# Scratch tensors re-laid: features with heads innermost, fewer and longer DMAs, shift rows issued by POOL

## The chip, the cores and the metric

One core of one Trainium2 chip runs the whole kernel. The metric is the device time of one execution in microseconds. TensorE (PE), VectorE (DVE), ScalarE (ACT), GpSimd (POOL) and SyncE (SP) run their own instruction streams and meet by semaphores. DMAs are issued by a queue of SP, ACT or POOL and moved by 16 DMA engines.

## The reference

A decoder layer on 32 sequences of 128 tokens, 128 features, 16 heads of 8. First a linear attention block, then cross attention to 77 context tokens, then a mixture of experts. The change touches the cross attention:

```python
def _feature_map(x, fm_w, fm_b):
    z = jnp.einsum('nshd,ed->nshe', x, fm_w) + fm_b
    return jnp.concatenate([jnp.exp(z), jnp.exp(-z)], axis=-1)   # 16 features per head
...
v, k, q = (_feature_map(x, fm_w, fm_b) for x in (v, k, q))
scores = jnp.einsum('nqhd,nkhd->nhqk', q, k) / jnp.sqrt(jnp.float32(EMBED))
attn = jax.nn.softmax(scores, axis=-1)
out = jnp.einsum('nhql,nlhd->nqhd', attn, v)
out = out.reshape(N, S, HEADS * EXP_DIM)
return out @ fc_w.T + fc_b
```

## The kernel before

`decoder_layer` has four phases, each with one function per engine. Phase 1 is the first attention block. The sequences are taken in groups of four (`JP`, `NG` = 8 groups).

**Phase 2, features.** For each group PE transposes the context and multiplies context and tokens with `map_w`; ACT takes the exponentials of K and then of Q, each as f32 and as bf16, in two halves (`hf`) of 8 heads with 16 features each on the 128 partitions, and copies the values to `vals` (line 547). Each feature is kept as three bf16 parts (high, middle, low): VectorE makes the parts of Q (`qpart`, semaphores `qhi`, `qmid`, `qlo`), POOL those of K (`kpart`; `khi`, `kmid`, `klo`). The buffers exist twice (`par`, the group's parity), so ACT may write a part of group g only when group g-2's DMA has left it (`k_sent`, `q_sent`). SP sends the parts to scratch in DRAM (`qparts`, `kparts`): per group six DMAs for K (line 473: two halves, three parts) and two for Q (line 478), in runs of 616 and 1,024 bytes.

**Phase 3, attention.** Sequences go in pairs (`JA` = 2, `NA` = 16 pairs). The scores are a sum over pairs of parts: `Q_PART` = (0, 0, 0, 1, 1, 2) meets `K_PART` = (0, 1, 2, 0, 1, 0), so 6 x 16 = 96 rows (`ROWS`) of `qst` and `kst`. `load_parts` fills them from scratch, transposed to 16 features on the partitions and heads along the row: per pair six DMAs of 128 KB for Q (line 629, every copy of a part by itself, 16 rows in runs of 512 bytes) and three for K (line 632, runs of 308 bytes). Four buffers (`NBUF`) take turns. PE computes the scores of pair g+2 (line 666, three units of heads) while it attends pair g; VectorE takes the row maxima, splits them in three parts (`parts`), PE turns them (line 675), ACT copies them to `mT` (line 838), and SP copies them as three further rows, the shift rows, to `qst` by two DMAs (line 640). Then PE computes the scores again with 99 rows, which subtracts the maximum (line 696), ACT takes the exponential (line 853), PE multiplies with the values (line 711), turns and projects (lines 728, 734, 740). `body(g)` of PE waits for the shift rows of its pair (`m_in`) and, in its first unit, for the loads of pair g+2 (`parts_in`). POOL copies each sequence's values (line 870) and adds the bias `fcb` to all of `xs` at once (line 874).

SP's order: writes of groups 0 to 5 each behind their context load; then loads of pairs 0 and 1 and the writes of groups 6 and 7 alternately; shift rows of pair 0; loads of pairs 2 and 3; then for each pair the load of pair g+3 (behind `bp`, the scores of pair g-1) and the shift rows of pair g+1. Phase 4, the experts, follows on all engines.

## Time and profile before

| | |
|---|---|
| median of 3 runs | 672.51 us (663.89 to 672.9) |
| the profiled execution | 663.64 us, its span 661.8 us |
| mean granted TensorE clock | 0.863 of 2.4 GHz |
| busy: PE, DVE, ACT, POOL | 474.3, 341.8, 253.9, 190.8 us |
| DMA | 101,485 packets, 61.94 MB, mean 94 GB/s |

Busy times are sums over an engine's instructions. "DMA share" is the mean share of the 16 DMA engines that were moving a packet; it can pass 1 where packets of several queues overlap. "PEclk" is the granted clock as a part of 2.4 GHz.

### The profile page before, as it was taken

Reading aid. Unit: us, or ns where it says so; the run is one execution under the profiler, and the core shown is the slowest. Engines: PE = TensorE matmul, PEld = TensorE weight load, DVE = VectorE, ACT = ScalarE, POOL = GpSimd, SP = SyncE. Lnnn points to the kernel's source line nnn. Section 1 sums busy time; section 2 is a strip of 40 time slices with the busy share of each in tenths; the row PEclk is TensorE's granted clock in tenths of the full one; section 3 lists DMA queues with packets and bytes.
Section 4 is the critical chain, followed back from the end, with each engine's and each line's share of the span. In section 5 each row is a group of like instructions: output and inputs, shape, how many; then the busy total and the mean of one; then the engine's idle time right before and its main releaser. Section 6 shows DMA issues by size and latency. Waiting matters only on the chain.

```text
span 661.8 us, 11782 instructions
## 1 busy us (share of the span) xinstructions
PE 474.3 (72%) x3778; PEld 317.1 (48%) x3778; DVE 341.8 (52%) x969; ACT 253.9 (38%) x578; POOL 190.8 (29%) x223
## 2 busy tenths in 40 slices
PE   0588888777771259998888888859894188988860
PEld 0255555544441136665655656534562055766650
DVE  4567755616759325555675676464830032334343
ACT  0445545358780024333443444536630022323220
POOL 3132222357787000000000000011047600455560
PEclk9999999988885557677987899969897689899895
DMA  5820000003669998989898994000031101556639
GB/s 96 295 76 1 0 0 1 0 11 115 200 190 161 178 122 92 97 90 104 92 119 87 104 113 44 2 1 1 0 125 53 49 0 33 150 178 203 203 102 254
DMA packets 101485, 61.94 MB, mean 94 GB/s; under 512 B 33832, under 2 KB 99656, under 8 KB 101320
## 3 DMA queue, kind: packets, MB, share of 16 engines
q1 hardware_dynamic: 91976, 52.92, 45.9%
q0 software_dynamic: 2560, 5.31, 2.3%
q10 hardware_dynamic: 6912, 3.25, 2.1%
q8 instruction: 19, 0.31, 0.2%
q14 instruction: 18, 0.15, 0.1%
HBM read 40.34 MB, written 20.73 MB: 92 GB/s over the span
## 4 chain that ended last, share of the span: by engine, by line
PE 42%; DVE 15%; SPq 12%; ACT 8%; issue 8%; another core or an unknown queue 6%; DMA 6%; POOL 1%; ACTq 1%; DVEq 0%; POOLq 0%
SPq L473 5%; PE bank L711 4%; PE bank L696 4%; PE bank L1204 3%; PE bank L1214 3%; ACT prob L853 3%; PE bank L1215 2%; PE bank L1263 2%; PE bank L734 2%; DMA qst<-mT 2%; PE bank L740 2%; PE bank L666 2%; PE bank L728 2%; SPq L629 2%
## 5 line engine op out<-in xcount | busy, mean ns | idle before, releaser
L853 ACT ACTIVATE prob<-bank 77x512 f32<-77x512 f32 x128 | 73.5, 591 | 111.6 <-PE bank L696 111.1
L870 POOL COPY vcur<-vals 77x272 f32 (+1 forms) x32 | 13.2, 416 | 192.6 <-PE bank L711 192.6
L711 PE MATMUL bank<-prob,vcur 77*17 77x128 f32 x1024 | 58.6, 305 | 12.5 <-ACT prob L853 12.1
L1178 POOL DMA_INDIRECT routed<-t_y,t_no x48 | 45.9, 956 | 71.6 <-DVE t_y L1047 59.9
L778 DVE TENSOR_REDUCE mx<-bank 128x5 f32<-128x385 f32 (+1 forms) x96 | 53.6, 579 | 24.3 <-PE bank L666 22.4
L666 PE MATMUL bank<-kst,qst 96*128 96x77 bf16 x512 | 40.9, 225 | 32.8 <-DMA kst<-kparts 27.6
L696 PE MATMUL bank<-qst,kst 99*77 99x128 bf16 x512 | 57.9, 244 | 7.8 <-DMA qst<-mT 6.6
L696 PEld LDWEIGHTS bank<-qst,kst 99*77 99x77 bf16 x512 | 44.2, 132 | 18.3 <-issue 9.9
L825 DVE COPY avs_s<-bank 128x512 f32<-128x512 f32 x32 | 22.1, 692 | 59.2 <-PE bank L711 59.2
L941 DVE TENSOR_TENSOR act<-bank,s_g 128x512 f32<-128x512 f32 x24 | 16.5, 688 | 62.9 <-ACT s_g L1115 59.6
L666 PEld LDWEIGHTS bank<-kst,qst 96*128 96x128 bf16 x512 | 31.9, 115 | 35.6 <-DMA kst<-kparts 14.6
L1204 PE MATMUL bank<-sd,act 128*128 128x128 f32 x192 | 27.9, 291 | 28.8 <-DVE act L941 20.0
L1204 PEld LDWEIGHTS bank<-sd,act 128*128 128x128 f32 x192 | 26.4, 203 | 43.1 <-DVE act L941 24.2
L1173 POOL DMA_INDIRECT sorted_in<-h_rows,pos_s x32 | 30.8, 964 | 41.7 <-issue 41.7
L379 POOL TENSOR_TENSOR qkv<-qkv,rn 128x256 f32<-128x256 f32 x32 | 19.1, 629 | 76.4 <-DVE rn L297 76.4
L1115 ACT ACTIVATE s_g<-bank 128x512 f32<-128x512 f32 x24 | 14.2, 597 | 69.0 <-PE bank L1215 33.0
L1040 DVE TENSOR_TENSOR t_act<-bank,t_sg 128x128 f32<-128x128 f32 x48 | 14.0, 291 | 48.4 <-ACT t_sg L1132 24.5
L1128 ACT COPY t_hT<-bank 128x128 f32<-128x128 f32 x48 | 12.7, 265 | 57.2 <-PE bank L1254 31.8
L711 PEld LDWEIGHTS bank<-prob,vcur 77*17 77x17 f32 x1024 | 17.5, 99 | 35.7 <-ACT prob L853 23.6
L1263 PE MATMUL bank<-t_hT,t_w 128*128 128x128 f32 x96 | 21.9, 311 | 13.5 <-ACT t_hT L1128 9.1
L331 ACT ACTIVATE xn<-xs,ln_bias,ln_rstd 128x128 f32<-128x128 f32 (+1 forms) x64 | 26.4, 482 | 10.1 <-DVE ln_bias L279 9.8
L412 PE MATMUL bank<-wqkv,xnT 128*128 128x384 f32 x64 | 25.3, 543 | 5.7 <-ACT xnT L338 5.7
(178 smaller groups left out, 1066.6 us busy)
## 6 DMA issues: line engine op xcount, KB each, us to landing
qst<-qparts SPq DMA_DIRECT2D x96, 128.0 KB, 5.3
t_w<-in_expert_w SPq DMA_DIRECT2D x48, 192.0 KB
qparts<-qpart SPq DMA_DIRECT2D x16, 384.0 KB, 3.4
kparts<-kpart SPq DMA_DIRECT2D x48, 77.0 KB
kst<-kparts SPq DMA_DIRECT2D x16, 231.0 KB, 7.8
sorted_in<-fill SPq DMA_DIRECT2D x1, 3168.0 KB, 10.4
t_row<-sorted_in ACTq DMA_DIRECT2D x48, 66.0 KB
kst<-kparts SPq DMA_DIRECT2D x16, 154.0 KB, 8.1
```

The source lines that it names most:

```text
L331: i = a.activation(dst[:, j], x_of(g, j), ACT.Identity, scale=ln_rstd[k][:, j:j + 1], bias=ln_bias[k][:, j:j + 1])
L412: pe.matmul(bank[1 + j][:, 0:3 * D], xnT[par][:, j * P:(j + 1) * P], wqkv[:], start=True, stop=True).then_inc(s["qkvp"], 1)
L473: sp.dma_start(kparts[a, :, heads, bass.ds(g * JK, JK)].rearrange("e h t -> h e t"), kpart[par][hf][:, a]).then_inc(k_sent[par][hf], 16)
L666: i = pe.matmul(bank[n % 2][:, (h - h0) * KEYS:(h - h0 + 1) * KEYS], qst[r][0:ROWS, h, j * S:(j + 1) * S], kst[r][0:ROWS, h, j * KEYS:(j + ...
L696: i = pe.matmul(bank[2 + u % 2][0:KEYS, c * S:(c + 1) * S], kst[r][0:SHIFT_ROWS, h, j * KEYS:(j + 1) * KEYS], qst[r][0:SHIFT_ROWS, h, j * ...
L711: i = pe.matmul(bank[4][32 * c:32 * c + EX + 1, (u - 1) * P:u * P], av_lhs(g, r, j, 4 * (u - 1) + c), prob[(u - 1) % 2][:, c], start=True, ...
L778: v.tensor_reduce(mx[:, n // 3, h0:h1], bank[n % 2][:, 0:(h1 - h0) * KEYS].rearrange("p (h k) -> p h k", k=KEYS), AX.X, ALU.max).then_inc( ...
L853: a.activation(prob[u % 2][:].rearrange("p c t -> p (c t)"), bank[2 + u % 2][0:KEYS], ACT.Exp, scale=SCORE_SCALE).then_inc(s["expd"], 1)
L1173: p.indirect_dma_start(out=sorted_in, out_offset=bass.IndirectOffsetOnAxis(ap=pos[:, b:b + 1].bitcast(U32), axis=0), in_=h_rows[:, b], in_ ...
L1178: p.indirect_dma_start(out=routed, out_offset=bass.IndirectOffsetOnAxis(ap=t_no[r][:].bitcast(U32), axis=0), in_=t_y[r][:], in_offset=None ...
L1204: i = pe.matmul(bank[BK_DOWN[par]][:, j * D:(j + 1) * D], act[c][:, j * P:(j + 1) * P], sd[:, c], start=(c == 0 and j == 0), stop=(c == CH ...
L1263: pe.matmul(bank[2 + r % 2][:, 0:P], t_w[r][:, 0:FF], t_hT[r % 2][:], start=True, stop=True)
```

## The change

The features are laid out with heads innermost: partition = feature x 16 + head, the first half (`hf` = 0) all the exp(z), the second all the exp(-z). The host builds `fm_wT`, `fm_b`, `signs` and `signcol` for it, and the copy of the values in line 547 reads its bank with a stride of 16 elements. The scratch tensors get a leading dimension for the group, then part, feature, head, token. So a write of a half with all its parts is one DMA (4 per group), and a row of 16 heads is contiguous: 16 KB for Q and 9,856 bytes for K. `qst` and `kst` hold four sequences instead of two, in three buffers instead of four, the third in the memory of the feature stage's own buffers (`early`); that one may be filled only after all writes have left and PE's last transposes of that stage (`vp`). A load of a group is three DMAs for Q, in which the copies of a part come from one broadcast source, and three for K. SP loads group 0 at turns 2 (Q) and 3 (K) of the feature stage and group 1 at turns 5 and 6, group 2 behind all writes, group G behind the scores of group G-3. The shift rows go to POOL's queue, ahead of the value copies; the bias is added by sequence; a memset of the third buffer's rows of ones is done by POOL between the first and the second shift. The loops of SP in the feature stage and of all engines in attention are written out.

```diff
-    NBUF = 4
+    NBUF = 3
...
-        qparts = nc.dram_tensor("qparts", (HEADS, EX, PARTS, TOK), BF16).ap()
-        kparts = nc.dram_tensor("kparts", (PARTS, EX, HEADS, B * KEYS), BF16).ap()
+        qparts = nc.dram_tensor("qparts", (NG, PARTS, EX, HEADS, GT), BF16).ap()
+        kparts = nc.dram_tensor("kparts", (NG, PARTS, EX, HEADS, JK), BF16).ap()
...
+            def body(g):
+                par = g % 2
+                for hf in range(2):
                     sp.wait_ge(s["klo"], g * 2 + (hf + 1))
-                    for a in range(PARTS):
-                        sp.dma_start(kparts[a, :, heads, bass.ds(g * JK, JK)].rearrange("e h t -> h e t"),
-                                     kpart[par][hf][:, a]).then_inc(k_sent[par][hf], 16)
+                    sp.dma_start(kparts[g, :, hf * HD:(hf + 1) * HD].rearrange("a e h t -> (e h) a t"),
+                                 kpart[par][hf][:]).then_inc(k_sent[par][hf], 16)
                 for hf in range(2):
-                    heads = slice(hf * HALF, (hf + 1) * HALF)
                     sp.wait_ge(s["qlo"], g * 2 + (hf + 1))
-                    sp.dma_start(qparts[heads, :, :, bass.ds(g * GT, GT)].rearrange("h e a t -> (h e) a t"),
+                    sp.dma_start(qparts[g, :, hf * HD:(hf + 1) * HD].rearrange("a e h t -> (e h) a t"),
                                  qpart[par][hf][:]).then_inc(q_sent[par][hf], 16)
...
+            for g in range(NG):
+                if g < NG - 2:
+                    sp.wait_ge(s["ctxTp"], g + 1)
+                    ctx_load(g + 2, g % 2)
+                if g == 2:
+                    sent(0, 1)
+                    load_q(sp, 0)
+                if g == 3:
+                    load_k(sp, 0)
+                if g == 5:
+                    sent(1, 2)
+                    load_q(sp, 1)
+                if g == 6:
+                    load_k(sp, 1)
+                body(g)
...
+        stage = [sb3, sb3, early()]
+        qst = [place(f"qst{i}", [SHIFT_ROWS, HEADS, GT], BF16) for i, place in enumerate(stage)]
+        kst = [place(f"kst{i}", [SHIFT_ROWS, HEADS, JK], BF16) for i, place in enumerate(stage)]
...
-        def load_parts(sp, g, r):
-
+        def load_q(sp, group):
+
+            r = group % NBUF
             for at, part, n in Q_RUNS:
-                for i in range(n):
-                    sp.dma_start(qst[r][(at + i) * EX:(at + i + 1) * EX],
-                                 qparts[:, :, part, bass.ds(g * JA * S, JA * S)].rearrange("h e t -> e h t")).then_inc(parts_in[r], 16)
+                same = qparts[group, part].rearrange("(o e) h t -> o e h t", o=1).broadcast_to([n, EX, HEADS, GT])
+                sp.dma_start(qst[r][at * EX:(at + n) * EX], same).then_inc(parts_in[r], 16)
+
+        def load_k(sp, group):
+
+            r = group % NBUF
             for at, part, n in K_RUNS:
                 sp.dma_start(kst[r][at * EX:(at + n) * EX],
-                             kparts[part:part + n, :, :, bass.ds(g * JA * KEYS, JA * KEYS)].rearrange("a e h t -> (a e) h t")).then_inc(parts_in[r], 16)
+                             kparts[group, part:part + n].rearrange("a e h t -> (a e) h t")).then_inc(parts_in[r], 16)
...
+            all_sent(sp, NG // 2)
+            sp.wait_ge(s["vp"], NG)
+            load_q(sp, 2)
+            load_k(sp, 2)
+            for group in range(3, NG):
+                sp.wait_ge(s["bp"], (group - 2) * (2 * 4 * JA))
+                load_q(sp, group)
+                load_k(sp, group)
...
+            shift(0)
             p.wait_ge(s["xn2"], NG)
-            p.tensor_tensor(xs[:], xs[:], fcb[:].rearrange("p (o f) -> p o f", o=1).broadcast_to([P, B, D]),
-                            ALU.add).then_inc(s["xb2"], 1)
+            for b in range(2 * JA):
+                add_bias(b)
+            all_sent(p, NG // 2)
+            p.wait_ge(s["vp"], NG)
+            p.wait_ge(s["xb2"], 2 * JA)
+            p.memset(kst[NBUF - 1][ROWS:SHIFT_ROWS], 1.0).then_inc(s["ones_rows"], 1)
+            p.wait_ge(s["ones_rows"], 1 + NBUF)
+            for g in range(NA):
+                if g < NA - 1:
+                    shift(g + 1)
+                for j in range(JA):
+                    b = g * JA + j
+                    if b + 2 * JA < B:
+
+                        p.wait_ge(s["avp"], 4 * (b + 1))
+                        copy_values(b + 2 * JA, b % (2 * JA))
+                        add_bias(b + 2 * JA)
```

`shift(g)` on POOL waits for `mT` of pair g and issues the same two DMAs as SP's did; `home(g, j)` gives a pair's buffer and place in it.

## Rows read from the trace of the kernel before

**Rows 1.** The page's chain that ended last, shares of the span by engine

```profile
PE 42%; DVE 15%; SPq 12%; ACT 8%; issue 8%; another core or an unknown queue 6%; DMA 6%; POOL 1%; ACTq 1%; DVEq 0%; POOLq 0%
```

**Rows 2.** Windows: busy us (x instructions) per engine, granted clock, DMA share, GB/s

```profile
144.00:200.00 56.00, 41.05 (x156) 24.68 (x156) 32.89 (x44) 44.98 (x89) 42.00 (x48) 0.86 0.51 154
200.00:239.00 39.00, 6.81 (x69) 4.68 (x69) 21.40 (x27) 0.95 (x3) 11.40 (x6) 0.51 1.14 171
239.00:437.40 198.40, 172.70 (x2315) 121.04 (x2315) 118.64 (x344) 85.18 (x175) 11.48 (x28) 0.84 0.80 83
384.00:400.00 16.00, 12.74 (x206) 9.07 (x207) 10.77 (x31) 7.19 (x16) 1.23 (x3) 1.00 1.19 113
```

**Rows 3.** The chain in order of time: start us, us, what

```profile
151.39 0.81 SPq L473
...
198.50 0.34 SPq L629
...
231.81 7.19 DMA kst<-kparts
```

**Rows 4.** Timeline of ACT, groups 4 and 7: start us, us, instruction

```profile
171.99 0.46 ACT L538 COPY ctxT_s<-bank 128x308 f32<-128x308 f32 x1
...
173.89 0.51 ACT L534 ACTIVATE kpart<-bank,map_b 128x308 bf16<-128x308 f32 x1
...
199.03 1.06 ACT L547 COPY vals<-bank 77x512 f32 x2
```

**Rows 5.** Timeline of SP, the K writes of group 1

```profile
159.26 4.79 SPq L473 DMA_DIRECT2D kparts<-kpart  x6
```

**Rows 6.** Window in attention: granted clock, DMA share, GB/s

```profile
276.00:286.00 10.00, 0.50 1.02 101
```

**Rows 7.** Waits between 250 and 437 us: us in total, times, longest

```profile
PE bank L696 <- DMA qst<-mT: 3.8, 5, 1.0
```

**Rows 8.** Timeline of ACT, the copies of the shift rows

```profile
217.85 0.27 ACT L838 COPY mT<-bank 128x128 bf16<-128x128 bf16 x1 [17.75 <-PE bank L675]
...
243.12 0.27 ACT L838 COPY mT<-bank 128x128 bf16<-128x128 bf16 x1 [0.98 <-PE bank L675]
...
386.30 0.27 ACT L838 COPY mT<-bank 128x128 bf16<-128x128 bf16 x1 [1.68 <-PE bank L675]
397.50 0.27 ACT L838 COPY mT<-bank 128x128 bf16<-128x128 bf16 x1 [0.58 <-PE bank L675]
...
418.63 0.27 ACT L838 COPY mT<-bank 128x128 bf16<-128x128 bf16 x1 [0.82 <-PE bank L675]
```

**Rows 9.** Short windows in a K write, a Q write, a shift copy: clock, DMA share, GB/s

```profile
154.20:154.30 0.10, 1.00 0.51 154
...
158.20:158.40 0.20, 1.00 0.95 353
...
420.40:420.50 0.10, 1.00 0.24 54
```

**Rows 10.** Window in a write of rows of 25 KB, the same columns

```profile
30.00:31.00 1.00, 1.00 0.94 406
```

**Rows 11.** The page's DMA issues: KB each, median us from issue to landing

```profile
qparts<-qpart SPq DMA_DIRECT2D x16, 384.0 KB, 3.4
```

**Rows 12.** Timeline of PE, the scores of pairs 0 and 1

```profile
211.04 0.88 PE L666 MATMUL bank<-kst,qst 96*128 96x77 bf16 x11 [13.43 <-DMA kst<-kparts]
...
224.44 0.90 PE L666 MATMUL bank<-kst,qst 96*128 96x77 bf16 x11 [6.63 <-DMA kst<-kparts]
225.74 2.28 PE L666 MATMUL bank<-kst,qst 96*128 96x77 bf16 x21 [0.41 <-DVE mx L778]
```

**Rows 13.** Single lines of POOL and ACT

```profile
L1178 POOL DMA_INDIRECT routed<-t_y,t_no x48: 952/957/960, 565.4 to 643.6; - x48
...
L547 ACT COPY vals<-bank x16: 573/593/624, 151.2 to 199.5; 77x512 f32 x12, 77x512 f32<-77x512 f32 x4
...
131.56 8.76 POOL L587 MEMSET kst<- 3x2464 bf16 x4
```

More of the change, by code:

```diff
@@ L525, in act_phase2, with features @@
         def act_phase2(a):
-            def features(g, par, g2, hf, z, f, part, zp, f_done, hi_done, lo, sent, loads):
+            def features(g, par, g2, hf, z, f, part, zp, f_done, hi_done, lo, sent):
                 a.wait_ge(s[zp], g * 2 + (hf + 1))
@@ L803, in tail @@
                 if stage == 2:
-                    if is_first(g) and j == 0:
-                        v.wait_ge(s["xb2"], 1)
+                    v.wait_ge(s["xb2"], b + 1)
                     v.wait_ge(s["fcp"], b + 1)
```

160 lines of the change are left out of this document (70 added, 90 removed).

## The prediction

> **What bounds the kernel now.** I read the chain that ended last first. No engine holds it: TensorE has 42% of the span, and SP's issuing 12%, an unusually large share for a queue [rows 1]. Then I cut the span into stages. Feature stage (144 to 200 us): ACT is busy for 45 of 56 us, VectorE for 33, POOL for 42. From 200 to 239 us TensorE does 6.8 us of work in 39. Attention (239 to 437.4) has TensorE busy for 173 of 198 us [rows 2]; the mixture of experts behind it takes the other 224 us and is not touched. The chain in order of time says what the 39 us are: SP starts line 473 at 151.4 and does not catch up; the first loads go out at 198.5, and the last that attention needs lands at 239 [rows 3]. ACT starts group 4 at 172.0 and ends group 7 at 200.1 with its last copy, 7.0 us per group of four sequences [rows 4]. SP takes 4.8 us for a group's six K writes, 0.8 each [rows 5]; with Q's two, the context load and waits it is 7.9 from the first group's start to the second's [rows 3, 5]. So the lag of SP's queue holds TensorE from about 200 to 239. In attention the DMA engines are full too (1.02 busy, 101 GB/s [rows 6]), but PE waits for DMA there in few places: 3.8 us for shift rows in the 16 pairs [rows 7]. The copies of the shift rows, one per pair of sequences, mark the pace: 11.2 us where the clock of 2.4 GHz is granted (1.00 from 384 to 400 [rows 2]); from 243.1 to 418.6 the mean of 14 pairs is 12.5 us, 25 per group [rows 8], with a mean clock of 0.84 [rows 2].
>
> **Part 1, the writes: 8 DMAs per group become 4.** SP per group: 4 of 0.8 us instead of 8 [rows 5], 3.2 us against ACT's 7.0. SP leaves the path; ACT's 7.0 us pace is left and the stage itself gains nothing that I count. What comes back is the lag afterwards. The new writes have 128 rows as outermost dimension, in runs of 1,024 and 616 bytes as before, so the bytes cost no more.
>
> **Part 2, the loads, and this is where I think the change fails.** A load of three copies of one part is one DMA whose source is (3 copies, step 0) x 16 rows x 16 KB, and the two-copy one has 2 outermost. How many of the 16 DMA engines does such a DMA use? The rows of before answer by shape. While only scratch writes of K run (outermost dimension 8 heads), a tenth of a microsecond shows 0.51 of the engines busy, half of 16; a Q write (outermost 128) shows 0.95 at 353 GB/s; the shift rows (3 destination rows outermost) show 0.24, 3 to 4 engines [rows 9]. So the outermost count limits the engines: three engines move 786 KB, and two move 524 KB. A rule speaks against this very form. The Trainium skill ("DMA: Bandwidth & Descriptors", section "Rules for kernel authors") says that a leading zero-stride broadcast of c copies confines the DMA to at most c engines, and its section "Why a DMA increments its semaphore by 16 and not by 1" says that these are the lowest-numbered ones. The trace's half and quarter agree; by that rule the sum is the one below, without it rival (b).
>
> What does the busiest engine carry for a group? One part is 16 x 16 KB = 262 KB. It carries one copy of the three, one of the two, 1/16 of the single one (16 KB), and 1/16 of K's 946 KB (59 KB). That both DMAs begin at the same engine no row shows; I take it, since one queue cuts up both, and a start elsewhere takes the two-copy share off (rival (a)). Rate of one engine: at best 406/(0.94 x 16) = 27 GB/s [rows 10]; where three engines each write one row of SBUF it is 54/(0.24 x 16) = 14 GB/s [rows 9]; with 16 engines on 16 rows it is 101/(1.02 x 16) = 6.2 [rows 6], but then 101 GB/s in total, which two or three engines don't reach, so I leave that out. I take 14 for the three-engine DMA, the nearest row, and 27 for the two-engine one, whose rows are long (16 KB against 256 bytes): 18.7 + 9.7 + 0.6 + 2.2 = 31.2 us per group. Both at 27: 22.2. Both at 14: 40.2. The Trainium skill ("SBUF — State Buffer", section "Door 1: The DMA port swizzle") puts partitions 32 apart on the same port, so copies one and three (rows 0 to 15 and 32 to 47) share one port's 27 GB/s and the two-copy DMA does not; an estimate from that page is 19.3 + 9.7 us in place of 18.7 + 9.7. No row shows it by itself. A load lands about 2.3 us after its bytes (a Q write lands in 3.4 [rows 11], of which 384 KB at 353 GB/s are 1.1).
>
> *In the feature stage.* The loads go into the same queue as the writes, ahead of them. The Q load of group 0 is issued in turn 2, about 163 (group 1's writes start at 159.3 [rows 5], and 4 take 3.2 us). It fills the first engine for 18.7 + 9.7 + 0.6 = 29 us. Group 2's writes, just behind, land at 163 + 29 + 2.3 = 194. Group 4's K features use the same buffer and wait for that: ACT wanted it at 173.9 [rows 4]. Delay 20 us, and behind ACT wait VectorE, POOL and TensorE. Then again: the Q load of group 1 goes out about 8 us after ACT resumes (202), the writes of group 5 behind it land at 202 + 29 + 2.3 = 234, and group 7's features, due at 194 + 3 x 7 = 215, wait for them. ACT ends the stage at 234 + 5 = 239 instead of 200.
>
> *At the start of attention.* Scores of the first pair start at 211.0 and its shift rows are copied at 217.9 [rows 8, 12]; the second pair takes 3.6 us more (224.44 to 228.02 [rows 12]); with 1 us for the shift rows' landing 11.5 us, so attention starts at 250. But group 2's load waits for all writes (239 + 5 = 244) and takes 31.2 + 2.3 + 0.5 to issue: 278. The scores of group 2 are due at the first pair of group 1, at 250 + 25 = 275. So group 1 starts at 278.
>
> *In attention.* Load G is issued when group G-3's last scores with shift are done, which I put 1.5 us ahead of group G-2's start (the last of eight score blocks of 11.2/8 us), and is needed when group G-1 starts: one group of time, 25 us, and this 1.5, against 33.5. Not hidden: groups 2 to 6 each start 33.5 - 1.5 = 32 us after the one before, 5 x 32 = 160, so group 6 starts at 438. From there to the end before took from about 393.4 (4.1 ahead of the copy at 397.5, as between 239.0 and 243.1 [rows 3, 8]) to 437.4, 44 us. End of attention 482, some 44 us later than before.
>
> **Part 3, shift rows on POOL.** Two issues per pair leave SP and go to POOL. The trace has no direct copy there; the nearest row is an indirect one, 957 ns [rows 13]. 1.9 + 2.3 = 4.2 us from copy to landing, against 11.2 - 4.1 = 7.1 between the copy and the next pair. POOL has 11 us of work in the 198 of attention [rows 2], and what queues behind it, the value copies, is wanted a pair later. No cost; at best the 3.8 us of waits [rows 7] go. If the cover goes, each microsecond late costs 15.
>
> **Part 4, the rest.** The bias add on POOL becomes 32 pieces; VectorE waits for a piece that is four sequences ahead: nothing. A memset twice as long as before, 4.4 us (8.76 for four [rows 13]), stands on POOL before the second shift, hidden by the first pair. The copy of values reads PSUM with a stride of 16 elements; the contiguous one takes 593 ns [rows 13]. No row shows such a read on ACT; from 0 to twice the time, 1.2 us per group or 9.5 us; I take 0, hidden by the stalls above. Unrolled loops: 0 to -3 us. Heads innermost is renamed columns otherwise.
>
> **Sum.** 663.6 (span 661.8 and 1.8 around it) + 44 = 708 us for the profiled execution. The median of the runs is 672.5, 9 us above that; part of this lies outside the stretches that the loads would set, so I give 712.
>
> **Rivals.** (a) The few engines run at 27 GB/s each, or the two broadcast DMAs fall on different engines (18.7 + 0.6 + 2.2 = 21.5 us). Group 4 waits to 185, the stage ends at 221, attention starts at 233; a load takes 24.5 us against 25, just hidden; 233 + 198 = 431, 6 us earlier than before: 657. For it: long rows, and the 14 comes from 256-byte ones. Against: it is the best row of the trace, and leaves no reserve. The point from which the load decides is 24 us on the busiest engine. (b) The change does what it says: the loads spread over 16 engines (a lowering that puts the 16 rows outside would do it). Then the stage ends at about 199, attention starts at 211 and lasts 198: 409, 28 us earlier, 635, or 630 with less waiting. Against it stand all three shapes [rows 9]. (c) 14 GB/s for both: first stall to 203, stage end near 259, load 42.5 us, 5 x 41: 782. (d) Shift rows issued on POOL are late, by 3 us a pair if an issue costs 3 us: 45 us on top of (b), hidden in my forecast. The Trainium skill ("SBUF — State Buffer", section "SBUF: two separate sides") warns that POOL can't write its descriptors while VectorE holds the shared port; no row here shows a direct copy on POOL.
>
> **How the numbers follow.** Forecast, with 27 to 34 us per group on the busiest engine, 690 to 736: 0.52. (a) 0.20; between (a) and the forecast 0.05; (b) 0.14; (c) 0.07; (d) 0.02. From 652 to 736 only (b), (c) and edges are left out, 2 in 10. A measurement of this kernel tells 2% from no change. Faster by more than that: (b) and an edge of (a), 0.18. Within: the rest of (a), 0.20. Slower: 0.62.
>
> **What would show it.** Windows during a Q load in attention: a DMA share of 0.2 or less at 40 to 60 GB/s, where before it was 1.02 at 101. ACT idle for some 20 us near 174 to 194, ended by a K write. TensorE waiting 6 to 8 us at the start of each of groups 1 to 6, ended by a DMA. I am wrong if the DMA share stands near 1 with over 150 GB/s during loads (b), or if the waits are there in the feature stage but not in attention (a).

## The result and the profile after

The changed kernel takes 739.65 us (median of 4 runs, 734.32 to 744.69); the kernel before, on the same chip, 669.61 (4 runs, 663.89 to 672.9). The ratio is 1.106 with a 95% interval of 1.093 to 1.118: slower, as forecast, but above the range, which ended at 736. Some executions of this program, whatever the kernel, are some per cent longer at a lower granted clock: medians here are over all runs, ratios and their intervals compare only the others. The profiled execution took 744.69 us, 742.9 of it span; the forecast for it was 708. So 33 us of loss are missing in the sum beside the 44 it had, and some 3 us lie behind attention (227.5 us against 224.4).

The page's chain that ended last, after; against [rows 1] SP's issuing falls from 12% to 2% and DMA rises from 6% to 19%:

```profile
PE 42%; DMA 19%; DVE 11%; ACT 8%; another core or an unknown queue 7%; issue 6%; POOL 4%; SPq 2%; ACTq 1%; DVEq 0%; POOLq 0%
```

Windows of the same stages (columns as in [rows 2]): features, the gap before attention, attention from its first score matmul with shift rows:

```profile
144.00:243.80 99.80, 42.95 (x158) 26.61 (x156) 36.07 (x45) 44.88 (x89) 42.95 (x47) 0.71 0.53 141
243.80:266.80 23.00, 5.99 (x65) 4.27 (x65) 15.83 (x26) 0.27 (x1) 11.35 (x13) 0.50 0.70 154
266.80:515.40 248.60, 215.75 (x2319) 151.01 (x2319) 121.13 (x343) 87.07 (x176) 41.29 (x86) 0.64 0.26 58
```

The feature stage lasts 100 us instead of 56 with the same busy time of ACT (44.9 against 45.0). What was 39 us of SP's lag is 23. Attention lasts 249 us. Before, it was 198 from 239.0, or 207 from its first score matmul with shift rows at 230.85, behind which TensorE waited 7.6 us for the K rows of pair 2. Its DMA share fell from 0.80 to 0.26, and TensorE's granted clock from 0.84 to 0.64.

ACT's timeline, where [rows 4] shows no such stop (idle before and its releaser in brackets), and the first copies of the shift rows (compare [rows 8]):

```profile
195.67 0.52 ACT L545 ACTIVATE kpart<-bank,map_b 128x308 bf16<-128x308 f32 x1 [22.01 <-DMA kparts<-kpart]
239.20 0.52 ACT L545 ACTIVATE kpart<-bank,map_b 128x308 bf16<-128x308 f32 x1 [21.75 <-DMA kparts<-kpart]
242.75 1.05 ACT L558 COPY vals<-bank 77x512 f32 x2
252.10 0.27 ACT L851 COPY mT<-bank 128x128 bf16<-128x128 bf16 x1 [8.30 <-PE bank L688]
271.34 0.27 ACT L851 COPY mT<-bank 128x128 bf16<-128x128 bf16 x1 [0.98 <-PE bank L688]
286.60 0.27 ACT L851 COPY mT<-bank 128x128 bf16<-128x128 bf16 x1 [1.44 <-PE bank L688]
302.87 0.27 ACT L851 COPY mT<-bank 128x128 bf16<-128x128 bf16 x1 [1.44 <-PE bank L688]
```

SP's timeline shows the cause of these two stops from the queue's side. The Q loads of groups 0 and 1 are issued in 2 us each. Then the issue of the next two Q writes, each 0.65 us in the median, takes 25 and 24 us together: SP itself is held up behind a load. Below them are the Q loads of groups 2, 3 and 4:

```profile
162.73 2.01 SPq L650 DMA_DIRECT2D qst<-qparts  x3
166.87 25.02 SPq L482 DMA_DIRECT2D qparts<-qpart  x2
...
206.77 1.85 SPq L650 DMA_DIRECT2D qst<-qparts  x3
211.06 23.96 SPq L482 DMA_DIRECT2D qparts<-qpart  x2
...
252.17 1.87 SPq L650 DMA_DIRECT2D qst<-qparts  x3
294.75 1.84 SPq L650 DMA_DIRECT2D qst<-qparts  x3
328.79 1.84 SPq L650 DMA_DIRECT2D qst<-qparts  x3
```

Windows of 2 us in the stall of group 4 and during the load of group 3, issued at 294.75 (granted clock, DMA share, GB/s):

```profile
176.00:178.00 2.00, 1.00 0.21 57
302.00:304.00 2.00, 0.50 1.01 179
308.00:310.00 2.00, 1.00 0.20 59
310.00:312.00 2.00, 1.00 0.17 49
326.00:328.00 2.00, 0.50 0.05 21
```

Some 10 us after the issue all engines are still full, and K pieces go through. Then 0.17 to 0.20 of 16 engines are left, that is three, at 49 to 59 GB/s in all, and at the end one (0.05 of 16). The trace's semaphore events give the last landing of each load: 330.4 for this one, 35.7 us after its issue; over the six loads in attention it is 34.9 to 36.5 us.

PE's timeline holds what my sum had as nothing: the scores with shift wait for the shift rows, at pair 0 and at the second pair of each of groups 1 to 5 (pairs 3, 5, 7, 9, 11). The copy for that second pair is issued some 9 us after the group's load. The chain in order of time has the same transfers with their whole length, issue to landing:

```profile
266.81 0.65 PE L709 MATMUL bank<-qst,kst 99*77 99x128 bf16 x4 [11.34 <-DMA qst<-mT]
...
314.74 0.64 PE L709 MATMUL bank<-qst,kst 99*77 99x128 bf16 x4 [3.25 <-DMA qst<-mT]
...
349.88 0.65 PE L709 MATMUL bank<-qst,kst 99*77 99x128 bf16 x4 [4.30 <-DMA qst<-mT]
...
383.93 0.65 PE L709 MATMUL bank<-qst,kst 99*77 99x128 bf16 x4 [6.23 <-DMA qst<-mT]
```

```profile
253.52 13.24 DMA qst<-mT
...
304.05 10.65 DMA qst<-mT
...
338.08 11.76 DMA qst<-mT
...
372.15 11.74 DMA qst<-mT
```

In total (waits of the whole span: us, times, longest) it is 32.3 us, against 3.8 in [rows 7], which leave out the first pair (6.6 with it):

```profile
PE bank L709 <- DMA qst<-mT: 32.3, 6, 11.3
```

No matmul of attention waits for a load. But the loads of groups 3, 4 and 5 land at 330.4, 364.3 and 399.8 us, and TensorE needs them when groups 2, 3 and 4 start, at 331.0, 366.2 and 400.2: the loads are only just hidden.

So there were two things to test. My theory, call it A: the broadcast loads on few engines explain the loss. A rival, call it B (the expectations below use A and B in senses of their own, given there): the shift rows, now beside the loads on another queue instead of in order with them on SP's, are late, and would be even with loads on all engines.

### The profile page after: what moved, and what is told of

Same layout as the page of the kernel before. It is cut to its first block, busy times and chain, and to the rows that moved or that the text cites. A ratio compares the mean times of both kernels' runs of the same rounds, so it can differ in the third digit from the quotient of the medians.

```text
span 742.9 us, 10825 instructions
## 1 busy us (share of the span) xinstructions
PE 517.3 (70%) x3778; PEld 347.9 (47%) x3778; DVE 342.2 (46%) x969; ACT 254.8 (34%) x578; POOL 221.3 (30%) x285
## 4 chain that ended last, share of the span: by engine, by line
PE 42%; DMA 19%; DVE 11%; ACT 8%; another core or an unknown queue 7%; issue 6%; POOL 4%; SPq 2%; ACTq 1%; DVEq 0%; POOLq 0%
DMA qst<-mT 9%; DMA kparts<-kpart 8%; PE bank L709 6%; PE bank L724 5%; PE bank L679 3%; PE bank L741 3%; PE bank L753 3%; PE bank L1239 2%; PE bank L747 2%; ACT prob L866 2%; PE bank L1298 2%; PE bank L1249 2%; PE bank L1250 2%; DVE ss L290 1%
## 5 line engine op out<-in xcount | busy, mean ns | idle before, releaser
L866 ACT ACTIVATE prob<-bank 77x512 f32<-77x512 f32 x128 | 75.0, 592 | 153.7 <-PE bank L709 153.7
L709 PE MATMUL bank<-qst,kst 99*77 99x128 bf16 x512 | 70.8, 284 | 32.3 <-DMA qst<-mT 32.3
L709 PEld LDWEIGHTS bank<-qst,kst 99*77 99x77 bf16 x512 | 55.6, 161 | 46.1 <-DMA qst<-mT 33.5
L724 PE MATMUL bank<-prob,vcur 77*17 77x128 f32 x1024 | 69.9, 358 | 9.2 <-ACT prob L866 8.2
L1213 POOL DMA_INDIRECT routed<-t_y,t_no x48 | 46.0, 958 | 75.3 <-DVE t_y L1082 64.2
L893 POOL DMA_DIRECT2D qst<-mT x32 | 19.7, 618 | 120.4 <-ACT mT L851 120.4
L679 PE MATMUL bank<-kst,qst 96*128 96x77 bf16 x512 | 49.1, 254 | 5.9 <-DVE mx L792 3.6
L1239 PEld LDWEIGHTS bank<-sd,act 128*128 128x128 f32 x192 | 26.4, 203 | 44.6 <-DVE act L976 23.7
L570 DVE TENSOR_TENSOR res_q<-qkv,qpart 128x512 f32<-128x512 f32 x16 | 14.9, 935 | 67.2 <-ACT qpart L545 67.1
L679 PEld LDWEIGHTS bank<-kst,qst 96*128 96x128 bf16 x512 | 40.6, 136 | 7.8 <-DVE mx L792 5.3
L530 PE MATMUL bank<-ident_s,kf 128*77 128x128 f32 x64 | 10.2, 312 | 41.3 <-ACT kf L542 41.3
L883 POOL COPY vcur<-vals 77x272 f32<-77x272 f32 x32 | 14.2, 448 | 81.3 <-PE bank L724 81.2
```

The lines of the kernel that those rows point to most:

```text
L679: i = pe.matmul(bank[n % 2][:, (h - h0) * KEYS:(h - h0 + 1) * KEYS], qst[r][0:ROWS, h, c * S:(c + 1) * S], kst[r][0:ROWS, h, c * KEYS:(c + ...
L709: i = pe.matmul(bank[2 + u % 2][0:KEYS, c * S:(c + 1) * S], kst[r][0:SHIFT_ROWS, h, t * KEYS:(t + 1) * KEYS], qst[r][0:SHIFT_ROWS, h, t * ...
L724: i = pe.matmul(bank[4][32 * c:32 * c + EX + 1, (u - 1) * P:u * P], av_lhs(g, j, 4 * (u - 1) + c), prob[(u - 1) % 2][:, c], start=True, st ...
L866: a.activation(prob[u % 2][:].rearrange("p c t -> p (c t)"), bank[2 + u % 2][0:KEYS], ACT.Exp, scale=SCORE_SCALE).then_inc(s["expd"], 1)
L893: p.dma_start(qst[r][ROWS:SHIFT_ROWS, :, c * S:(c + 1) * S], mT[g % 2][at:at + PARTS * HEADS]).then_inc(m_in[r], 16)
L1213: p.indirect_dma_start(out=routed, out_offset=bass.IndirectOffsetOnAxis(ap=t_no[r][:].bitcast(U32), axis=0), in_=t_y[r][:], in_offset=None ...
```

## The experiments

They ran in five sets, on chips on which the kernel before takes 630.46, 680.48, 632.16, 673.86 and 679.96 us; each ratio is to the kernel before of the same set, and times of different sets are not compared. Each edit is to the changed kernel unless another is named. A kernel with one run has a ratio without an interval. The changed kernel itself came to 1.106 on one chip and 1.079 on another, so ratios of different sets can differ by 0.03 for that reason alone. Changes to semaphore counts that follow from an edit are left out of the cuts. The expectation written before each run stands ahead of its result. "Landing" is the median and the longest time from issue to landing of the 32 shift-row DMAs.

**Set 1: where the copies stand, and whose queue.**

*Each copy its own DMA*, 16 feature rows outermost:

```diff
-                same = qparts[group, part].rearrange("(o e) h t -> o e h t", o=1).broadcast_to([n, EX, HEADS, GT])
-                sp.dma_start(qst[r][at * EX:(at + n) * EX], same).then_inc(parts_in[r], 16)
+                for i in range(n):
+                    sp.dma_start(qst[r][(at + i) * EX:(at + i + 1) * EX], qparts[group, part]).then_inc(parts_in[r], 16)
```

> The changed kernel with each copy of a Q part loaded by a DMA of its own (six Q DMAs per group instead of three, outermost dimension 16 rows; all else as in the changed kernel). Theory A (the broadcast source with 3 or 2 copies outermost confines the load to 3 or 2 DMA engines; that makes the stalls of the feature stage, the late shift rows and the slow attention): no stall of ACT near 174 us, DMA share near 1 during a load at 100 GB/s or more, a load done within 20 us, attention starts near 212 us, time 630 to 650 us. Rival B (the long rows or the group-wise buffers themselves are slow, or the shift rows on POOL's queue are late by that queue): the stalls remain, time stays above 700 us.

Measured: 687.27 us, 1.080 (1.066 to 1.095). The stops of ACT for K writes fall from 44.5 to 17.7 us, the longest from 22.0 to 8.2, but shift rows land after 2.7 (median) to 14.9 us, and the waits for them grow from 32.3 to 46.6. The time lies between what the two theories gave.

*The same bytes with the feature row outermost and the copies inside it*:

```diff
-                same = qparts[group, part].rearrange("(o e) h t -> o e h t", o=1).broadcast_to([n, EX, HEADS, GT])
+                same = qparts[group, part].rearrange("e (o h) t -> e o h t", o=1).broadcast_to([EX, n, HEADS, GT])
...
-                             kparts[group, part:part + n].rearrange("a e h t -> (a e) h t")).then_inc(parts_in[r], 16)
+                             kparts[group, part:part + n].rearrange("a e h t -> e a h t")).then_inc(parts_in[r], 16)
```

> The changed kernel with the same six loads per group, but the rows of qst and kst ordered feature first and copy second, so that each load's source has the 16 features outermost and the copies inside. Same bytes, same number of DMAs, same run lengths. Theory A (engine count set by the outermost dimension): as good as single copies or better, since 48 rows are written at once: load at 200 GB/s or more, done in some 12 us, time 625 to 645 us. Rival B (a broadcast source or long runs are slow by themselves): above 700 us.

Measured: 659.81 us, 1.046 (1.035 to 1.058). Windows during its load, issued at 264.45, and PE's timeline at the same load:

```profile
270.00:272.00 2.00, 1.00 0.99 197
278.00:280.00 2.00, 0.91 0.94 193
280.00:282.00 2.00, 0.50 0.22 36
```

```profile
236.50 0.65 PE L709 MATMUL bank<-qst,kst 99*77 99x128 bf16 x4 [10.37 <-DMA qst<-mT]
...
283.43 0.65 PE L709 MATMUL bank<-qst,kst 99*77 99x128 bf16 x4 [5.42 <-DMA qst<-mT]
```

So the outermost count does limit the engines: with 16 outside, the share goes from 0.2 to about 1 and the rate from 49 to 59 to between 113 and 197 GB/s (windows from 266 to 280), and the load lands 18.8 us after its issue instead of 35.7. The stops of ACT are down to 13.4 us, the longest 5.9. The first attention matmul comes at 236.5 instead of 266.8. This is the rule that the Trainium skill states in "DMA: Bandwidth & Descriptors", "Rules for kernel authors" (a leading zero-stride broadcast of c copies uses at most c engines); the share of 0.17 to 0.20 with three copies agrees. But the kernel is still slower than before, above the 625 to 645 us expected, and PE waits 29.3 us for shift rows: theory A doesn't hold alone.

*Shift rows issued from ACT's queue* instead of POOL's, loads as changed:

```diff
                 a.copy(mT[g % 2][:], bank[5][:, 256:256 + S // 2].bitcast(BF16)).then_inc(s["mT"], 1)
+                a.wait_ge(s["mT"], g + 1)
...
+                    a.dma_start(qst[r][ROWS:SHIFT_ROWS, :, c * S:(c + 1) * S], mT[g % 2][at:at + PARTS * HEADS]).then_inc(m_in[r], 16)
```

> The changed kernel with the shift rows issued from ACT's queue right behind the copy, instead of from POOL's. Theory A (the shift rows land late because their 256-byte pieces share DMA engines with 16 KB pieces of the load and take turns with them): they land as late as before, 10 to 13 us behind the issue during a load, time 730 to 750 us. Rival C (POOL's software queue is what makes them late): they land within 4 us, attention starts 10 us earlier and each group of four is some 2 to 5 us shorter, time 705 to 720 us.

Measured (one run): 835.96 us, 1.326. No theory had this time. PE waits for shift rows in 64.2 us between 200 and 460, the longest at the first pair:

```profile
292.70 0.65 PE L709 MATMUL bank<-qst,kst 99*77 99x128 bf16 x4 [31.50 <-DMA qst<-mT]
```

So POOL's queue alone is not what makes them late: another queue made it worse. The packets in the traces say more. On ACT's queue the two copies of a pair go as 96 packets of 256 bytes on three engines, and behind the load they leave one by one: from 288.2 us on, the packets start 0.63 us apart, the time that the fastest of the load's 16 KB packets take (0.61 us). So each small piece lets one large piece go first, which is the turn-taking that theory A of this run names, only much dearer than its 10 to 13 us. The shift rows arrive with the end of the load: TensorE goes on at 292.7 and 359.2 us, the loads' last landings are at 294.2 and 359.3. On POOL's queue the same two copies are six packets of 4,096 bytes and 26 of 64, and 32 of 4 bytes besides, that is 16 for each DMA. So the two queues cut the same copy differently, and this run changes more than the queue.

*Each Q load cut in four by heads*, copies still outermost:

```diff
+                for h in range(0, HEADS, 4):
+                    same = qparts[group, part, :, h:h + 4].rearrange("(o e) h t -> o e h t", o=1).broadcast_to([n, EX, 4, GT])
+                    sp.dma_start(qst[r][at * EX:(at + n) * EX, h:h + 4], same).then_inc(parts_in[r], 16)
```

> The changed kernel with each Q load cut in four by heads, so that one piece is 4 KB instead of 16 KB; still on 3 and 2 engines, same bytes. Theory A (shift rows wait for one piece of the load per piece of their own): they land about 4 times sooner, in some 5 us instead of 12 during a load; attention starts near 258 us instead of 267; a load still takes some 32 us, so the groups still follow each other at 32 to 33 us at best: time 715 to 735 us. Rival (the load's duration alone sets the pace and the shift rows only end last by the profile): 735 to 750 us, unchanged.

Measured (one run): 680.0 us, 1.079. That is 35 us below the range expected. Waits for shift rows fall to 5.8 us, landing 3.1 to 10.4; 16.0 us of waits for K loads come in. Smaller pieces or the slower issue (13 us for a Q load's twelve DMAs) help the shift rows even on few engines.

**Set 2: without shift rows at all.** The kernel before and the changed one were run again on this chip.

> The kernel before, unchanged, for its profile on the chip of this set. Both theories: attention in some 190 to 205 us, the granted clock of TensorE 0.8 or more in it, pairs of 11 to 13 us.

> The changed kernel, unchanged, timed on the chip of this set, since chips differ. Ratio to the kernel before 1.09 to 1.13, as on the first chip.

Measured: 676.26 us and 733.35 (1.079, 1.071 to 1.088). Both expectations were missed by a little: the kernel before had a clock of 0.78 in attention, and the ratio lies below 1.09 and clear of the first chip's interval. The start of attention is the same as on that chip (266.8), but attention takes 233 us there at a clock of 0.73, against 249 at 0.64. So some 15 us of the first result go with the clock that was granted. The changed kernel waits here 24.6 us for shift rows and 11.0 for K loads:

```profile
PE bank L709 <- DMA qst<-mT: 24.6, 6, 11.1
PE bank L679 <- DMA kst<-kparts: 11.0, 3, 6.1
```

*No shift copies*. These two kernels leave the three shift rows out of the scores, so that the softmax has no maximum taken off, and scale the exponent by 1/1000:

```diff
-                                          kst[r][0:SHIFT_ROWS, h, t * KEYS:(t + 1) * KEYS],
-                                          qst[r][0:SHIFT_ROWS, h, t * S:(t + 1) * S], start=True, stop=True)
+                                          kst[r][0:ROWS, h, t * KEYS:(t + 1) * KEYS],
+                                          qst[r][0:ROWS, h, t * S:(t + 1) * S], start=True, stop=True)
...
-                pe.wait_ge(m_in[home(g, 0)[0]], shifts(g))
...
-                    p.dma_start(qst[r][ROWS:SHIFT_ROWS, :, c * S:(c + 1) * S], mT[g % 2][at:at + PARTS * HEADS]).then_inc(m_in[r], 16)
```

> The changed kernel without the copies of the shift rows and without TensorE's wait for them (the second scores take 96 rows, so the maximum is not subtracted, and the exponential is taken at a thousandth of the scale so that it stays finite; POOL still waits for the same copy of ACT). The loads on 3 and 2 engines are left. Theory A (late shift rows cost some 13 us at the start of attention and about 5 per group; behind them the load itself, 33 us against one group of time, limits the pace): start some 12 us earlier, groups still 31 to 33 us apart, 15 to 30 us less than the changed kernel. Rival (the shift rows only end last and the load would hold everything as long): within 8 us of the changed kernel. Rival (the shift rows alone make attention slow): 50 us or more less.

Measured (one run): 725.53 us, 1.066, only 8 us below the changed kernel's median and 2.5 below its fastest run, so the rival of my expectation (within 8 us) held. The load itself is what comes next (waits between 200 and 460, and PE's timeline at the first of them; the load was issued at 253.50):

```profile
PE bank L679 <- DMA kst<-kparts: 35.7, 3, 15.6
```

```profile
294.10 0.57 PE L679 MATMUL bank<-kst,qst 96*128 96x77 bf16 x6 [10.32 <-DMA kst<-kparts]
```

The waits are the same in sum, 35.7 us against 24.6 + 11.0: they only moved from the shift rows to the load. Attention starts at 256.4 instead of 266.8 and ends 5 us earlier.

*No shift copies and the feature outermost*, both edits above:

> The loads of the run with features outermost (16 engines), and the shift rows left out as in the run without shift rows. Theory A (with loads on 16 engines only the shift rows' lateness is left): no wait of TensorE for a DMA in attention, pairs of 11 to 12 us at full clock, attention in some 180 to 190 us, 5% or more below the kernel before. Rival (something else, such as the granted clock by itself, keeps pairs at 15 us): attention in 230 us and more, above the kernel before.

Measured (one run): 657.93 us, 0.967. Nothing in attention waits for a DMA, and its first matmul comes at 222.34:

```profile
222.34 0.63 PE L709 MATMUL bank<-qst,kst 96*77 96x128 bf16 x4
```

So there are two costs that lie one above the other: with few engines the load holds attention and the late shift rows add little; with 16 engines the load is hidden and the shift rows hold it, from 0.967 to 1.046 (ratios of two sets). In the two profiles attention ends 43 us later with shift rows: it starts 14 us later, waits 19 us more inside, and the other 10 go with a lower clock, which no run takes apart from the waits.

**Set 3: what makes the shift rows late.** All but the last are edits to the kernel with the feature outermost.

*Every load cut in four by heads*, 24 DMAs per group with pieces of 4 KB or less:

```diff
+                for h in range(0, HEADS, 4):
+                    same = qparts[group, part, :, h:h + 4].rearrange("e (o h) t -> e o h t", o=1).broadcast_to([EX, n, 4, GT])
...
+                for h in range(0, HEADS, 4):
...
+                                 kparts[group, part:part + n, :, h:h + 4].rearrange("a e h t -> e a h t")).then_inc(parts_in[r], 16)
```

> Features outermost (16 engines), and each load cut in four by heads: pieces of 4 KB for Q and 2.4 KB for K, 24 DMAs per group, the shift rows from POOL as in the changed kernel. Theory A (a shift row's piece waits for one piece of the load at each turn): shift rows land within 5 to 6 us during a load instead of 12, TensorE's waits for them shrink to 0 to 2 us, ratio to the kernel before 0.97 to 1.00 (features outermost alone: 1.046). Rival (it is the load's burst as a whole and not the size of its pieces): they land with the end of the load as before, ratio 1.03 to 1.06.

Measured: 615.07 us, 0.973 (0.962 to 0.985): below the kernel before, though the interval doesn't exclude a gain under 2%. Landing 2.9 to 7.4 us, waits for shift rows 7.0. The issue of a load is now spread over 15 us (SP's timeline), and from 229 to 420 us, inside attention, the clock is 0.80:

```profile
252.28 7.01 SPq L651 DMA_DIRECT2D qst<-qparts  x12
259.34 7.70 SPq L658 DMA_DIRECT2D kst<-kparts  x12
```

```profile
229.00:420.00 191.00, 170.89 (x2226) 120.34 (x2218) 113.62 (x334) 80.75 (x168) 41.30 (x86) 0.80 0.45 75
```

*The load waits until the next pair's shift rows have landed*:

```diff
                 sp.wait_ge(s["bp"], (group - 2) * (2 * 4 * JA))
+                g = 2 * (group - 2)
+                sp.wait_ge(m_in[home(g + 1, 0)[0]], shifts(g + 1))
                 load_q(sp, group)
```

> Features outermost, and SP holds each group's load back until the shift rows of the next pair have landed, so that only one of a group's two shift copies can meet a load. Theory A: shift rows land in 2 to 3 us at the first pair, but the load then runs into the second one's copy or ends late: between the two, ratio 0.98 to 1.03. Rival (shift rows are late for another reason): 1.04 or more.

Measured: 639.86 us, 1.016 (1.008 to 1.024), as expected; waits 13.2 us in place of 29.3, landing 2.8 to 10.4.

*The shift rows row by row*, six DMAs per pair with 16 heads outermost in place of two with 3 rows outermost:

```diff
+                    for a in range(PARTS):
+                        p.dma_start(qst[r][ROWS + a:ROWS + a + 1, :, c * S:(c + 1) * S],
+                                    mT[g % 2][at + a * HEADS:at + (a + 1) * HEADS]).then_inc(m_in[r], 16)
```

> Features outermost with the long pieces, and the shift rows copied one destination row at a time: six DMAs per pair with 16 heads outermost instead of two with 3 rows outermost, so that each of 16 engines carries one piece of each instead of three engines 16. Theory A (each piece waits its turn behind a long piece, so 16 pieces in a row on an engine make the 10 to 12 us): they land in 3 to 5 us plus 2.5 us more of issuing, no waits of TensorE over 2 us in attention, ratio 0.96 to 0.99, near the run without shift rows (0.97). Rival (the queue serves the software queue only when the load is through): waits as with features outermost alone, 1.04 to 1.06.

Measured: 664.4 us, 1.054 (1.045 to 1.064); landing 1.9 to 15.0, waits 36.4; 0.96 to 0.99 was expected. On more engines they are no sooner there.

*The three-copy load split into two and one* (on the changed kernel; this tests the 14 GB/s of my sum):

```diff
+                for i, m in ((0, 2), (2, 1)) if n == 3 else ((0, n),):
+                    same = qparts[group, part].rearrange("(o e) h t -> o e h t", o=1).broadcast_to([m, EX, HEADS, GT])
+                    sp.dma_start(qst[r][(at + i) * EX:(at + i + m) * EX], same).then_inc(parts_in[r], 16)
```

> The changed kernel with the three-copy load split into a two-copy and a one-copy DMA, so that no three engines write rows 0 to 15 and 32 to 47 at once; the busiest engine carries the same two copies as before. If an engine writes at 14 GB/s only where three write (as in the forecast's sum), the busiest engine's share of a load falls from 31 or more to 22 to 24 us: DMA share near 0.13 at 50 to 54 GB/s (27 per engine) in the middle of a load, groups 27 to 31 us apart instead of 33 to 34, held by the shift rows alone. If the rate of an engine into one row is 14 anyway: share 0.13 at 28 GB/s, a load of 40 us, groups 38 us apart, slower than the changed kernel.

Measured (one run): 676.92 us, 1.071. Window in its load:

```profile
302.00:304.00 2.00, 0.50 0.12 49
```

Two engines (0.12 of 16) carry 49 GB/s, 24.5 each; the three of the changed kernel carried 49 to 59, 16 to 20 each in the mean. Their packets of 16 KB show that the mean is of two kinds: in the changed kernel, between 266 and 270 us, one stream of packets takes 0.61 us each (27 GB/s) and two take mostly 1.25 to 1.30 us (12.6 to 13 GB/s); here, between 298 and 315, both streams mostly take 0.61 to 0.66. So the rates of my expectation hold, but its time for a load doesn't: the busiest engine was to need 22 to 24 us, and the loads in attention land 33.5 to 38.4 us after their issue, the first 10 us with all engines busy. TensorE waits 17.3 us for K loads, where I expected waits for shift rows alone (13.4).

**Set 4: size or time of the pieces.** *Loads cut in two* (as above with 8 heads, 12 DMAs per group):

> Features outermost with each load cut in two by heads: pieces of 8 KB for Q and 4.9 KB for K. Theory A (lateness follows the size of the load's pieces: 16 KB gave up to 12.3 us from issue to landing, 4 KB up to 7.4): between the two, up to 9 to 11 us, TensorE's waits for shift rows between 7 and 30 us in sum. Rival (cutting at all helps, by pacing SP's issues): as with 4 KB, up to 7.5 us and waits of 7 us.

Measured (one run): 684.45 us, 1.016; landing 2.5 to 11.3, waits 26.4. Cutting in two hardly helps, as the theory of piece size had it.

*Pieces of 1 KB without more DMAs* (616 bytes for K), on the kernel with a DMA for each copy:

```diff
+                    sp.dma_start(qst[r][(at + i) * EX:(at + i + 1) * EX], qparts[group, part],
+                                 max_dma_last_dim=1024).then_inc(parts_in[r], 16)
```

> Each copy of a Q part by a DMA of its own (16 rows outermost), runs cut to 1,024 bytes for Q and 616 for K: 9 DMAs per group of four where the kernel before has 18. Theory A: shift rows land within 4 to 5 us, no waits of TensorE over 1 us; the load itself is slower than with features outermost, since 16 engines write 16 rows (about 20 us per group), and still hidden: ratio 0.95 to 0.98. Rival (the number of turns and not the size of the pieces): landing up to 12 us, ratio 1.03 or more.

Measured: 716.22 us, 1.066 (1.055 to 1.078); landing 2.5 to 14.0, waits 39.5. Windows at the end of the load issued at 268.33, and PE's timeline:

```profile
288.00:290.00 2.00, 0.50 0.96 139
290.00:292.00 2.00, 0.50 0.03 5
```

```profile
289.10 0.65 PE L710 MATMUL bank<-qst,kst 99*77 99x128 bf16 x4 [7.24 <-DMA qst<-mT]
```

The shift rows land as the load ends (its last landing is at 291.3), as they did with large pieces and the feature outermost (PE goes on at 283.4 there, the load's last landing is at 283.2). For POOL's queue, the theory that a small copy waits only for large pieces ahead of it falls.

*Four pieces and the load held back* (both edits of set 3):

> Pieces of 4 KB, features outermost, and each load held back until the shift rows of the next pair have landed. Theory A (what is left of the waits, 7 us, comes from the overlap of the load's start with the first shift copy): waits 0 to 4 us, ratio 0.96 to 0.97. Rival (holding the load back only moves the overlap to the second copy, as in the run with long pieces, where 13 us were left): ratio 0.975 to 0.99.

Measured: 671.52 us, 0.997 (0.991 to 1.003). Waits for shift rows 2.8 us, landing 2.6 to 6.4; 4.1 us of waits for K loads. Fewer waits did not bring a shorter time than four pieces alone: attention takes 207 us here against 203 there (first score matmul with shift to last projection). Each load is issued later here, the one of group 3 at 8.7 us behind the start of group 1 instead of 2.2 ahead of it, but no run shows that this is the cause.

*The kernel before with its shift rows on POOL's queue* (POOL's loop of value copies is written out around them):

```diff
-                sp.wait_ge(s["mT"], g + 1)
...
-                    sp.dma_start(qst[r][ROWS:SHIFT_ROWS, :, j * S:(j + 1) * S], mT[r % 2][at:at + PARTS * HEADS]).then_inc(m_in[r], 16)
+            def shift(g):
+                p.wait_ge(s["mT"], g + 1)
...
+                    p.dma_start(qst[g % NBUF][ROWS:SHIFT_ROWS, :, j * S:(j + 1) * S], mT[g % 2][at:at + PARTS * HEADS]).then_inc(m_in[g % NBUF], 16)
```

> The kernel before with one edit: its shift rows issued from POOL's queue instead of SP's (and POOL's loop of value copies written out around them). Theory A (with pieces of 308 and 512 bytes in the load, the shift rows don't wait): they land in 2 to 4 us instead of 6.5, the 4 us of waits in attention go, and attention's first pair starts earlier, since the copy is no longer behind SP's backlog: it starts when the loads allow, ratio 0.98 to 1.00. Rival (the software queue is late beside any load): landing of 7 us or more, ratio above 1.00.

Measured: 683.47 us, 1.010 (0.995 to 1.026); landing 4.9 to 8.3, waits 8.0, where 2 to 4 us and no waits were expected. They are late beside the old loads as well, but moving the queue alone costs nothing that can be told from the time.

**Set 5: the fastest version again**, on the chip with 679.96 us for the kernel before (11 runs):

> The same kernel as features outermost with pieces of 4 KB, once more, on whatever chip this set gets. Theory A (the gain is the kernel's: TensorE starts attention some 15 to 20 us earlier and waits little in it): ratio 0.96 to 0.99. Rival (the gain was that chip's): 0.99 to 1.01.

Measured: 656.73 us, median of 6 (643.27 to 659.49). By the rule for ratios only the fastest of the six counts: 643.27 us against 673.84, the median of the five runs of the kernel before that count, 0.955 without an interval. It points the same way as the 0.973.

## Why the prediction went wrong in size

*Held: direction, and the mechanism of the loads.* A Q load on three engines (0.17 to 0.20 at 49 to 59 GB/s; forecast 0.2 or less at 40 to 60), ACT stopped for 22 us up to 195.7 (forecast 194), and again up to 239.2 (forecast 234), the stage's end at 243.8 (forecast 239). With 16 rows outermost the stops of 22 us were gone and the first attention matmul came 30 us earlier. Rivals (a), (b) and (c) are out: the load wasn't short enough to leave room, it didn't spread, and it landed after 34.9 to 36.5 us, not 42.5. One sign that I had named did not come: TensorE was to wait 6 to 8 us at the start of each group for the load. It waited 1.7 to 6.2 us at the second pair, for shift rows. Only without shift rows did it wait for K loads alone, 10 to 16 us at every second group.

*The step that failed* is part 3, "No cost", with its rival (d), which I put down as "hidden in my forecast". I took the landing of shift rows from a queue with nothing beside it, 2.3 us after an issue of 0.95. Issue was cheaper (0.62) and the median landing 3.4, but the landings that matter are those beside a load: 10.7 to 13.2 us. The trace of the kernel before already had a sign of it, which I didn't use, in its chain: a shift copy right behind a load took 6.5 us.

```profile
336.89 6.53 DMA qst<-mT
```

At the start of attention nothing hides it. Group 2's load goes out at 252.17 and the first shift rows at 252.68; the last land 13.2 us after their issue, and attention starts at 266.8 instead of 250, of which 5 are the feature stage's and 12 this. The cover between a copy and the next pair (7.1 us in my sum) was also too small at the second pair of groups 1 to 5, by 1.7 to 6.2 us.

*But this step alone is not the miss.* Taking the shift rows away gave back 8 us, because the load then held attention. The terms of the load were too small as well. I had 31.2 us for the busiest engine and 33.5 from issue to landing; measured are 34.9 to 36.5. In the first 10 us after the issue all engines are full, with K's pieces and the single copy, and the busy engines share in that (of the 15 packets of 16 KB that start between 255 and 256 us, 12 take 1.4 to 2.4 us and not 0.61); the sum had no term for it. And I had the load of group 2 issued at 244, where it went out at 252.2. The 14 GB/s of the three-copy load were near (two of the three streams at 12.6 to 13, the third at 27). The Trainium skill ("SBUF — State Buffer", "Door 1: The DMA port swizzle") puts partitions 32 apart on one port; that the same copies as two and one ran at 24.5 GB/s per engine agrees, though no run moved a copy to other rows to show it alone.

*And a clock that I had not followed through.* The granted clock of attention is 0.64 instead of 0.84. A pair at 0.50 takes 16.3 us, a pair at 1.00 takes 10.9. TensorE waited before its clock fell (1.00 from 308 to 314 us, a wait of 3.3 up to 314.7, then 0.70 and 0.50), but no run shows the waits as the cause: on another chip the same kernel with much the same waits had 0.73, and the kernel with 16 engines and without shift rows, with no wait for a DMA, had 0.79.

The budget of the missing 33 us, from the starts of the groups in PE's timeline: group 1 starts at 297.0 instead of 278, 19 us late, of which 10.7 are the load of group 2, landed at 288.7 (8.2 by its later issue, 2.5 by its length), and 8.3 the time from that landing to the start. These 8.3 I put down to the late shift rows; they agree with the 8 that taking the rows away gave back. Groups 1 to 5 take 170.9 us instead of 160; a load of 35.6 us (the mean of these five) that is issued 2.2 ahead of a group's start allows no less than 167. The last two groups take 47.5 instead of 44, with no load left; the clock is 0.50 at their start. With 3 behind attention it is the 36.7 of 744.7 - 708. Only with both the slow loads and the shift rows gone (0.967), or with both mended (0.973), does the change give what its idea could.

*Part 4* held: the strided read of PSUM takes 602 ns against 593 [rows 13], and part 1 too: SP's issuing left the chain (12% to 2%).

*Open.* Why shift rows from POOL's queue land late beside a load. On ACT's queue the traces show it: 256-byte pieces that alternate with 16 KB pieces. On POOL's they don't. The number of engines that carry the bytes is not it, since 16 heads outermost were no sooner there; nor is the size of the load's pieces alone, since 1 KB did as 16 KB did. In the changed kernel the last 4,096-byte packet of pair 0 starts at 261.1 us and the last of the 4-byte ones at 265.8: what ends late is not the data. There are 16 of these small packets for each DMA, by their number one for each engine, so it seems that such a copy ends only when the slowest of all 16 engines has served it. What helped is what spreads the load over time or holds it back (landing at most 7.4 and 10.4 us in place of 12.3), so I hold the length of the burst queued at once on each engine to be the cause, which is argued, not shown: 24 short DMAs differ from 6 long ones in size as well as in pace. A paced issue with long pieces wasn't tried.

## What to carry to other kernels

In a DMA with a broadcast source, put the rows outermost on both sides (16 here) and the copies inside them; three and two copies outermost ran on three and two engines, and what was queued behind them, the issuing engine included, stood still. A small copy that TensorE waits for must be costed beside the largest transfer that may be in flight (here 11 to 13 us), not by its landing with nothing beside it (2 to 3). If moving copies to a second queue removes the order between them and the loads, try the loads in pieces issued over time; here the kernel at 1.046 came to 0.973 with it. And when two transfers are both late, taking away one shows only what the other leaves: here 8 us, where the same copies cost some 40 once the loads were mended.

## What the runs showed that I had not expected

Shift rows issued on ACT's queue beside the changed loads kept TensorE waiting 31.5 us at the first pair, where POOL's queue had 11.3; ACT's queue cut them into 96 packets of 256 bytes, POOL's into six of 4,096 and some small ones. The issue of a single Q write, 0.65 us in the median, held SP for 11 to 14 us when the load ahead used few engines. Cutting the loads into 1 KB pieces cost little: with a DMA for each copy, the load of group 3 landed 23.0 us after its issue, against 21.8 with pieces of 16 KB.
